# A pre-norm attention and mixture-of-experts kernel on one core: GpSimd's scatters of the last two batches and the last batch's routing in another order, and each tile's two results sent one step sooner

## The chip, the cores and the metric

The kernel runs on one core of a Trainium2 chip. Five engines work side by side and wait for each other by semaphores: TensorE (PE, matmuls), VectorE (DVE), ScalarE (ACT), GpSimd (POOL) and SyncE (SP, which here only issues transfers). The metric is the device time of one execution in microseconds (us), lower is better.

## The reference

The input is four sequences of 1024 tokens of 128 numbers. A layer norm, an attention whose scores are the normalised rows times themselves (scaled by two vectors), and a residual; then a second layer norm and a mixture of 8 experts, of which each token uses two; and a second residual.

```python
x = x + attn(layernorm(x))            # softmax(lhs @ rhs^T) @ x, x: (4, 1024, 128)
xf = layernorm(x).reshape(4096, 128)
probs = softmax(xf @ router_w.T)      # 8 experts
topk_probs, topk_idx = top_k(probs, 2); topk_probs /= sum(topk_probs)
h = gelu(einsum('nc,ech->neh', xf, w_fc) + b_fc)     # hidden 512
out = einsum('neh,ehc->nec', h, w_proj) + b_proj
y = einsum('nec,ne->nc', out, combine)               # combine: the two gates, else 0
x = x + y
```

The kernel computes each token for its two experts alone.

## The kernel before, in words

The tokens are 32 groups of 128 rows, eight to a batch, and a batch (b = 0 to 3) is one sequence. Everything is unrolled code for each engine, with the order of its instructions written out by hand; there is no scheduler. An engine runs its list in order, so an instruction that waits holds back all that stand behind it.

**Attention.** For a batch, TensorE computes 16 blocks of scores (score), VectorE takes their row maxima (row_max), TensorE turns and subtracts them, ScalarE exponentiates (exponent), and TensorE sums the rows in 16 pieces (attend). The last two pieces need shift_again of VectorE and then exponent of ScalarE. While batch b is in work, what is left of batch b - 1 is done beside it: its second layer norm (take_stats2 and take_moments2 on VectorE, scale_ln2 on GpSimd with a power function, make_h2 and high_h2 on ScalarE, split_h2 on VectorE) and its routing.

**Routing.** VectorE finds the two best experts of each row (picks, 11 small steps and a last one that writes "taken"), and the gap of their logits (find_gap, which needs scale_ln2). TensorE counts ranks (rank_round) and VectorE keeps them (keep_ranks). GpSimd raises e to the gap (gate_powers). VectorE's find_slots writes each row's slot and its gates; in the middle it waits for gate_powers (gate_exp). There are five rounds: batch 0, batch 1, the two halves of batch 2 (rounds 2 and 3), batch 3 (round 4, "last"). Then GpSimd sends the rows to their slots in DRAM (dispatch(b, i), i from 0 to 15, an indirect DMA of 128 rows each, a scatter from here on). A dispatch waits for split_h2 of its half (h2lo_made) and find_slots of its round (meta_made). In batch 2 and, before the change, in batch 3, some scatters also wait for a certain maximum or exponent (dispatch_max, dispatch_next, dispatch_own with their PACE numbers), which spreads them.

**Experts.** 39 tiles of 256 slots follow. For tile k, SyncE loads the slots, TensorE turns them (turn_slots), ScalarE copies them (copy_xT), TensorE multiplies by the first weights (up, 12 matmuls), ScalarE does the gelu, TensorE multiplies by the second weights (down, 16 matmuls), VectorE adds the bias and applies the gates (add_bias, gate), and GpSimd sends the 256 results back with two indirect DMAs (give_back). In step k, TensorE does turn_slots(k + 2), up(k), down(k - 2), and VectorE keep_rows(k), add_bias(k - 3), gate(k - 3). up(k) counts the semaphore "stepped"; most engines are paced by it. Tiles 0 to 7 need batches 0 and 1 in their slots, tiles 8 to 15 also batch 2, the rest all. Which slots a tile has is computed by VectorE in three tables (steps(second_table, n) does the next n small steps of the second). In the first steps of this stage the end of the routing still runs: batch 3's round 4, scale_ln2(6) and scale_ln2(7), the scatters of batch 2 and of batch 3 (LAST_SCATTERS says before which step). At the end SyncE waits for all results, loads them, VectorE adds them to x, and SyncE stores.

TensorE goes into the experts after its last attend and a wait for the weights' low parts (low_part on GpSimd, three of them in the last batch).

## Time and profile before

| | us |
|---|---|
| median of 3 runs (lowest, highest) | 371.75 (371.2, 372.22) |
| the profiled execution's own time | 370.49 |
| its span, first to last instruction | 368.7 |
| TensorE busy with matmuls | 293.3 (80%) |
| VectorE, ScalarE, GpSimd busy | 222.1, 194.5, 185.7 |

The span lies 1.8 us below the time of its execution, and that execution 1.3 us below the median. Busy time of TensorE is of pipelined matmuls with modelled ends, so it shows when the engine had work, not that it ran at its best. Attention lasts until 174 us of the span, the experts from there to 347, and the final sum to the end. Times below are from the span's start.

### The profile page before, as it was taken

The numbers are of one execution on the slowest core, as the hardware profiler recorded it, in microseconds if no ns is written. First come the engines' busy times: TensorE is split into PE (matmuls) and PEld (weight loads), VectorE is DVE, ScalarE is ACT, GpSimd is POOL, SyncE is SP. The second block draws the span as 40 slices with busy tenths as digits, with TensorE's granted clock in tenths as the row PEclk, the third lists the DMA queues.
The fourth block names the chain that finished last, engine by engine and source line by source line (L and its number), as shares of the span: only waits on it lengthen the run. The fifth ranks groups of instructions, "written<-read, shape, count | busy, mean of one in ns | idle before, by whom it ended". The sixth has DMA issues, their size and how long they took to land.

```text
span 368.7 us, 7888 instructions
## 1 busy us (share of the span) xinstructions
PE 293.3 (80%) x2206; PEld 256.7 (70%) x2207; DVE 222.1 (60%) x890; ACT 194.5 (53%) x392; POOL 185.7 (50%) x247
## 2 busy tenths in 40 slices
PE   8989988999769994999699272999999999995000
PEld 3669985889558883788588161999999999995000
DVE  3759788888837887778667022665544544453055
ACT  4445557862635614746588022677776777772000
POOL 7011034543865137488786675456555655566300
PEclk9999999999998999999989776799999999999555
DMA  7920000030010001014213321023322222111198
GB/s 218 431 95 1 2 1 0 3 117 16 22 51 29 4 16 45 29 32 118 75 38 90 81 75 59 30 74 110 89 81 75 80 80 72 45 37 50 48 338 325
DMA packets 16948, 29.37 MB, mean 80 GB/s; under 512 B 3760, under 2 KB 12848, under 8 KB 16656
## 3 DMA queue, kind: packets, MB, share of 16 engines
q1 hardware_dynamic: 12080, 18.40, 15.5%
q0 software_dynamic: 4832, 10.53, 8.6%
q8 instruction: 17, 0.28, 0.3%
q14 instruction: 19, 0.16, 0.1%
HBM read 16.30 MB, written 12.62 MB: 78 GB/s over the span
## 4 chain that ended last, share of the span: by engine, by line
PE 60%; DVE 15%; issue 11%; DMA 4%; POOL 4%; ACT 3%; another core or an unknown queue 2%; SPq 1%; POOLq 0%; ACTq 0%; DVEq 0%
PE av_ps L1295 18%; PE av_ps L1094 12%; DVE neg_piece L1402 6%; PE sc_ps L1276 5%; PE sc_ps L1274 5%; PE sc_ps L1275 5%; DMA raw_proj<-results 3%; PE bank L1262 3%; POOL results L867 2%; PE bank L1079 1%; PE sc_ps L1083 1%; PE bank L1083 1%; PE bank L1070 1%; DVE stats L1445 1%
## 5 line engine op out<-in xcount | busy, mean ns | idle before, releaser
L867 POOL DMA_INDIRECT results<-prob,result_row x78 | 75.2, 964 | 57.1 <-PE sc_ps L1276 35.3
L1295 PE MATMUL av_ps<-raw_proj,raw_fc 128*128 x624 | 80.9, 284 | 10.1 <-issue 10.1
L768 POOL DMA_INDIRECT slots<-stage,slot x64 | 63.1, 987 | 45.7 <-DVE stage L1562 21.9
L1295 PEld LDWEIGHTS av_ps<-raw_proj,raw_fc 128*128 128x128 f32 x624 | 76.8, 200 | 10.6 <-issue 9.9
L1011 ACT ACTIVATE raw_fc<-sc_ps,bfc,scale_down 128x256 f32<-128x256 f32 x156 | 75.3, 570 | 2.3 <-PE sc_ps L1276 2.3
L1094 PE MATMUL av_ps<-h_all,prob 128*128 128x137 f32 x512 | 73.2, 287 | 0.0
L1094 PEld LDWEIGHTS av_ps<-h_all,prob 128*128 128x128 f32 x512 | 67.3, 192 | 3.6 <-DVE res L1430 1.1
L1731 DVE TENSOR_TENSOR h_all<-av_ps,bpr 128x256 f32<-128x256 f32 x39 | 16.6, 425 | 75.3 <-PE sc_ps L1276 43.6
L1003 ACT ACTIVATE h_all<-bank 128x512 f16<-128x512 f16 x39 | 23.2, 597 | 60.1 <-PE sc_ps L1276 32.6
L1274 PE MATMUL sc_ps<-h_all,wfc_hi 128*128 128x256 f16 x156 | 43.7, 280 | 2.7 <-issue 1.8
L1275 PE MATMUL sc_ps<-h_all,wfc_hi 128*128 128x256 f16 x156 | 43.7, 280 | 1.1 <-issue 1.1
L1276 PE MATMUL sc_ps<-h_all,wfc_lo 128*128 128x256 f16 x156 | 43.7, 280 | 0.8 <-issue 0.8
L1402 DVE TENSOR_REDUCE neg_piece<-bank 128x1 f32<-128x512 f32 x32 | 21.9, 686 | 16.7 <-remote 6.2
L916 ACT ACTIVATE prob<-sc_ps 128x512 f32<-128x512 f32 x32 | 18.4, 599 | 13.5 <-PE sc_ps L1083 11.3
L906 ACT ACTIVATE again<-bank 128x512 f32<-128x512 f32 x16 | 9.5, 594 | 29.1 <-DVE neg_piece L1402 25.7
L1402 DVE TENSOR_REDUCE neg_piece<-sc_ps 128x1 f32<-128x512 f32 x32 | 21.8, 684 | 0.8 <-issue 0.7
L1738 DVE TENSOR_SCALAR prob<-h_all,row_gate 128x128 f32<-128x128 f32 x78 | 21.5, 385 | 1.4
L1262 PE MATMUL bank<-ident,slots_in 128*128 128x128 f16 x156 | 16.0, 223 | 6.9 <-issue 5.9
L1274 PEld LDWEIGHTS sc_ps<-h_all,wfc_hi 128*128 x156 | 15.6, 100 | 5.2 <-issue 3.1
L1262 PEld LDWEIGHTS bank<-ident,slots_in 128*128 128x128 f16 x156 | 12.0, 99 | 10.1 <-issue 9.6
L1070 PE MATMUL bank<-hT_hi,q_hi 128*128 128x512 f32 x32 | 15.2, 475 | 4.7 <-ACT again L906 4.3
L1276 PEld LDWEIGHTS sc_ps<-h_all,wfc_lo 128*128 x156 | 15.7, 100 | 4.5 <-issue 2.3
(177 smaller groups left out, 516.7 us busy)
## 6 DMA issues: line engine op xcount, KB each, us to landing
slots_in<-slots SPq DMA_DIRECT2D x39, 132.0 KB
raw_fc<-in_w_fc_dram SPq DMA_DIRECT2D x1, 2048.0 KB, 11.2
raw_proj<-in_w_proj_dram SPq DMA_DIRECT2D x1, 2048.0 KB, 15.4
raw_fc<-results SPq DMA_DIRECT2D x2, 1024.0 KB, 7.1
raw_proj<-results SPq DMA_DIRECT2D x2, 1024.0 KB, 11.7
out_dram<-res SPq DMA_DIRECT2D x4, 512.0 KB, 5.0
res<-in_x_dram SPq DMA_DIRECT2D x3, 512.0 KB, 5.6
results<-prob,result_row POOLq DMA_INDIRECT x78
```

Of the source, the lines that this page charges most:

```text
L768: pool.indirect_dma_start(out=slots[:, :], out_offset=bass.IndirectOffsetOnAxis(ap=slot[:, n, k:k + 1], axis=0), in_=stage[:, b % 2, t, :] ...
L867: pool.indirect_dma_start(out=results[:, :], out_offset=bass.IndirectOffsetOnAxis(ap=result_row[a][:, h:h + 1], axis=0), in_=gated[a][h], ...
L1003: act.activation(xT[:, a % NH, :], bank[a % 2][:, :].bitcast(F16)[:, 0:2 * W], ACT.Copy).then_inc(xT_made, 1)
L1011: ins = act.activation(hid[:, a % NH, c, :], up_ps(a, c), ACT.Gelu_apprx_tanh, bias=bfc[:, e, c:c + 1], scale=scale_down[:, 0:1])
L1094: mm = pe.matmul(att[:, t, 0:AUG], probT[:, m % RING, t * P:(t + 1) * P], h_aug[:, b % 2, exp_rows(n), :], start=(n % BT == 0 and t % 2 == ...
L1262: mm = pe.transpose(o[:, part * W + h * P:part * W + (h + 1) * P], x, ident16[:, :])
L1274: pe.matmul(o, wfc_hi[:, e, w], xT[:, a % NH, 0:W], start=True, stop=False, skip_group_check=True)
L1275: pe.matmul(o, wfc_hi[:, e, w], xT[:, a % NH, W:2 * W], start=False, stop=False, skip_group_check=True)
L1276: mm = pe.matmul(o, wfc_lo[:, e, w], xT[:, a % NH, 0:W], start=False, stop=True, skip_group_check=True)
L1295: mm = pe.matmul(o, hid[:, a % NH, c, s], wpr[:, e, c, :], start=(c == 0 and h == 0), stop=(c == HC - 1), skip_group_check=True)
L1402: dve.tensor_reduce(neg_piece[:, r // TU, r % TU, c:c + 1], block_bank(n), AX_X, ALU.max, negate=True).then_inc(max_made, 1)
L1738: ins = dve.tensor_scalar(gated[k % NR][h], biased[:, a % NH, h, :], row_gate[:, a, h:h + 1], None, ALU.mult)
```

## The change

GpSimd's list in the last batch (b = 3): the scatters 5 to 15 of batch 1 no longer wait for maxima or exponents; the first scatters of batch 2 (0 to 7) stand before the weights' low parts instead of behind them; the second power of the gates (round 3) stands behind the low parts instead of ahead of them; scatters 8 to 15 of batch 2 stand in pairs between the remaining small operations. Batch 3's first eight scatters stand before step 4 instead of step 6, the second eight before step 6 instead of step 7. The results of tile k are sent in GpSimd's step k + 3 instead of k + 4. The last batch's routing: VectorE does all steps of picks at once, ahead of its last layer norm statistics and of the tiles; TensorE's rank_round stands behind up(1) instead of behind down(2); keep_ranks stands in step 1 and find_slots in step 2 instead of both in step 5; the second table and split_h2 move with them.

```diff
                 if b == B - 1:
-                    dispatch_max(b - 2)
+                    for i in range(len(PACE_OWN), SCATTERS - 4):
+                        dispatch(b - 2, i)
                     gate_powers(ROUNDS_BY[b - 1] - 2)
-                    dispatch_next(b - 2, 0)
+                    for i in range(SCATTERS - 4, SCATTERS):
+                        dispatch(b - 2, i)
+                    for i in range(2):
+                        dispatch(b - 1, i)
                 if b >= 1:
                     scale_ln2(2 * b - 1)
...
-                if b >= 2:
+                if b == 2:
                     dispatch_next(b - 2, 1)
-                if b >= 1:
-                    gate_powers(ROUNDS_BY[b - 1] - 1)
                 if b == B - 1:
+                    for i in range(2, SCATTERS // 2):
+                        dispatch(b - 1, i)
                     for i in range(EMPTY_PIECES, PIECES):
                         low_part(i)
+                if b >= 1:
+                    gate_powers(ROUNDS_BY[b - 1] - 1)
...
-            for i in range(5):
+            for i in range(8, 10):
                 dispatch(B - 2, i)
             scale_ln2(2 * B - 2)
-            for i in range(5, 11):
+            for i in range(10, 12):
                 dispatch(B - 2, i)
             scale_ln2(2 * B - 1)
-            for i in range(11, 15):
+            for i in range(12, 14):
                 dispatch(B - 2, i)
             gate_powers(len(ROUNDS) - 1)
-            for i in range(15, SCATTERS):
+            for i in range(14, SCATTERS):
                 dispatch(B - 2, i)
...
-            LAST_SCATTERS = {6: range(0, 8), 7: range(8, SCATTERS)}
+            LAST_SCATTERS = {4: range(0, 8), 6: range(8, SCATTERS)}
...
-                if k >= 4:
+                if k >= 3:
                     if tile_there(k):
                         pool.wait_ge(stepped, up_at(k))
-                    give_back(k - 4, (k - 4) % NR)
-            run_each_tile(no_experts, step, 4, lambda group: None)
+                    give_back(k - 3, (k - 3) % NR)
+            run_each_tile(no_experts, step, 3, lambda group: None)
...
             def down(k, a, of, last):
                 e = of
                 pe.wait_ge(gelu_done, k + 1)
-                if isinstance(k, int) and k == 0:
-                    pe.wait_ge(res_made, 2 * B)
-                    pe.wait_ge(lgpart_made, 2 * B)
-                if isinstance(k, int) and k == 3:
+                if isinstance(k, int) and k == 1:
                     pe.wait_ge(ranks_kept, len(ROUNDS))
...
                 if tile_there(k):
                     up(k, a)
+                if isinstance(k, int) and k == 1:
+                    pe.wait_ge(res_made, 2 * B)
+                    pe.wait_ge(lgpart_made, 2 * B)
+                    rank_round(len(ROUNDS) - 1)
                 if later(k, 2):
                     down(k - 2, (a - 2) % NB, expert[a - 2], not tile_there(k + 1))
-                if isinstance(k, int) and k == 4:
-                    pe.wait_ge(biased_made, 2)
-                    rank_round(len(ROUNDS) - 1)
...
             last = len(ROUNDS) - 1
-            choose = picks(last)
+            steps(picks(last), 2 * K * E)
+            take_stats2(2 * B - 1)
+            take_moments2(2 * B - 1)
...
-                if k == 0:
-                    take_stats2(2 * B - 1)
-                    take_moments2(2 * B - 1)
-                if 1 <= k < 4:
-                    steps(choose, (5, 5, 3)[k - 1])
-                if k == 3:
+                if k == 1:
                     find_gap(last)
+                    keep_ranks(last)
+                if k == 2:
+                    find_slots(last)
                     split_h2(2 * B - 2)
                 if k < 5:
-                    steps(second_table, (3, 4, 4, 2, 20)[k])
-                if k == 5:
-                    keep_ranks(last)
-                    find_slots(last)
-                if k == 7:
+                    steps(second_table, (3, 3, 3, 6, 20)[k])
+                if k == 6:
                     split_h2(2 * B - 1)
```

How GpSimd's list reads in the last batch, from the scatters of batch 1 on. L768 is a scatter into slots, L777 the gates' power (gate_powers), L728 to L737 one scale_ln2, L742 the low parts. Before:

```order
L768 DMA slots<-stage,slot 32768x132 x6
L777 TENSOR_TENSOR gate<-euler,gap 128x4
L768 DMA slots<-stage,slot 32768x132 x4
L728 TENSOR_SCALAR neg_mean<-moments 128x4
L734 TENSOR_TENSOR rstd<-var,minus_half 128x4
L737 TENSOR_TENSOR shift<-neg_mean,rstd 128x4
L768 DMA slots<-stage,slot 32768x132 x4
L777 TENSOR_TENSOR gate<-euler,gap 128x4
L742 TENSOR_TENSOR wfc_lo<-raw_fc,wfc_hi 128x512 x3
L768 DMA slots<-stage,slot 32768x132 x5
```

Of the change, the same place:

```order
L768 DMA slots<-stage,slot 32768x132 x10
L777 TENSOR_TENSOR gate<-euler,gap 128x4
L768 DMA slots<-stage,slot 32768x132 x6
L728 TENSOR_SCALAR neg_mean<-moments 128x4
L734 TENSOR_TENSOR rstd<-var,minus_half 128x4
L737 TENSOR_TENSOR shift<-neg_mean,rstd 128x4
L768 DMA slots<-stage,slot 32768x132 x6
L742 TENSOR_TENSOR wfc_lo<-raw_fc,wfc_hi 128x512 x3
L777 TENSOR_TENSOR gate<-euler,gap 128x4
L768 DMA slots<-stage,slot 32768x132 x2
```

Eight more scatters stand ahead of the second of these powers than before (22 instead of 14 from the list's first row on), and the low parts too.

GpSimd's list at batch 3's scatters, behind the last one of batch 2; L867, in the change L874, is a result sent back (give_back). Before:

```order
L768 DMA slots<-stage,slot 32768x132
L867 DMA results<-prob,result_row 20224x128 x4
L768 DMA slots<-stage,slot 32768x132 x8
L867 DMA results<-prob,result_row 20224x128 x2
L768 DMA slots<-stage,slot 32768x132 x8
L867 DMA results<-prob,result_row 20224x128 x72
```

Of the change:

```order
L768 DMA slots<-stage,slot 32768x132 x2
L874 DMA results<-prob,result_row 20224x128 x2
L768 DMA slots<-stage,slot 32768x132 x8
L874 DMA results<-prob,result_row 20224x128 x4
L768 DMA slots<-stage,slot 32768x132 x8
L874 DMA results<-prob,result_row 20224x128 x72
```

One tile's results moved from ahead of batch 3's first eight scatters to behind them. The rows don't show the step each group waits for: the first eight now stand before step 4, the second before step 6.

VectorE's list behind the second tile's keep_rows (its last row is L1724, in the change L1731): in between stands what precedes the third tile's. Before, picks and the second table (L484 to L493):

```order
L1724 TENSOR_TENSOR result_row<-chosen_row,spare_row 128x2
L1511 SCALAR_TENSOR_TENSOR lg<-pick,lg 128x64
L1494 TENSOR_REDUCE best<-lg 128x8
L1497 TENSOR_TENSOR pick<-lg,best 128x64
L1500 SCALAR_TENSOR_TENSOR pick<-pick,expert_id 128x64
L1504 TENSOR_REDUCE first_id<-pick 128x8
L484 TENSOR_REDUCE sums<-chosen 128x16
```

Of the change, find_slots and split_h2 (L1470):

```order
L1731 TENSOR_TENSOR result_row<-chosen_row,spare_row 128x2
L1549 TENSOR_TENSOR pick<-pick,rank 128x64 x2
L1552 TENSOR_REDUCE slot_f<-pick 128x8 x2
L1555 CAST slot<-slot_f 128x16
L1557 TENSOR_SCALAR gate_sum<-gate 128x8
L1561 RECIPROCAL stage<-gate_sum 128x8
L1563 TENSOR_TENSOR stage<-stage,gate 128x8
L1566 TENSOR_SCALAR stage<-first_id 128x8
L1567 COPY stage<-row_id 128x8
L1470 TENSOR_TENSOR stage<-h,stage 128x4x128
```

Before, find_slots stood behind two tiles' add_bias; now it stands ahead of the first tile's. L1557 is the row that waits for the gates' power.

## Rows read from the trace of the kernel before

**Rows 1.** The page: the chain that ended last, by engine.

```profile
PE 60%; DVE 15%; issue 11%; DMA 4%; POOL 4%; ACT 3%; another core or an unknown queue 2%; SPq 1%; POOLq 0%; ACTq 0%; DVEq 0%
```

**Rows 2.** Stretches: busy time and count of each engine, granted clock, DMA share.

```profile
205.00:210.00 5.00, 1.07 (x4) 0.39 (x3) 0.00 (x0) 0.00 (x0) 3.78 (x5) 0.73 0.33 80
...
260.00:300.00 40.00, 39.83 (x384) 37.87 (x383) 18.82 (x95) 28.63 (x60) 22.67 (x24) 1.00 0.29 82
```

**Rows 3.** Timeline of GpSimd (POOL), last batch: start, us, what, idle before.

```profile
138.79 1.07 POOL L768 DMA_INDIRECT slots<-stage,slot  x1 [0.54 <-issue]
...
146.24 1.05 POOL L777 TENSOR_TENSOR gate<-euler,gap 128x4 f32<-128x4 f32 x1
...
156.77 0.19 POOL L728 TENSOR_SCALAR neg_mean<-moments 128x4 f32<-128x4 f32 x1 [1.86 <-DVE moments L1453]
...
158.84 1.07 POOL L768 DMA_INDIRECT slots<-stage,slot  x1 [0.56 <-issue]
...
164.79 3.40 POOL L742 TENSOR_TENSOR wfc_lo<-raw_fc,wfc_hi 128x512 f16<-128x512 f32 x3
```

**Rows 4.** Timelines, last batch: ScalarE's copy of turned maxima; VectorE's find_slots, last shifts.

```profile
146.95 0.60 ACT L902 ACTIVATE neg_rows<-bank 128x512 fp32r<-128x512 f32 x1 [0.86 <-PE bank L1079]
...
154.33 0.68 DVE L1465 TENSOR_TENSOR stage<-h,stage 128x512 f16<-128x512 f32 x1
...
168.77 0.16 DVE L1552 TENSOR_SCALAR gate_sum<-gate 128x4 f32<-128x4 f32 x1
...
169.54 1.28 DVE L1407 TENSOR_TENSOR again<-again,bank 128x512 f32<-128x512 f32 x2
```

**Rows 5.** Timeline of TensorE, the last 64 matmuls of attention.

```profile
166.63 7.76 PE L1094 MATMUL av_ps<-h_all,prob 128*128 128x137 f32 x64
```

**Rows 6.** Timelines in batch 2: GpSimd, TensorE, ScalarE, VectorE.

```profile
96.37 1.08 POOL L768 DMA_INDIRECT slots<-stage,slot  x1 [0.55 <-issue]
...
106.64 0.96 POOL L768 DMA_INDIRECT slots<-stage,slot  x1 [0.30 <-issue]
...
103.15 0.48 PE L1083 MATMUL bank<-neg_rows,ones_r 128*128 128x512 f32 x1
...
107.86 0.60 ACT L916 ACTIVATE prob<-bank 128x512 f32<-128x512 f32 x1 [4.16 <-remote]
...
110.76 0.69 DVE L1402 TENSOR_REDUCE neg_piece<-bank 128x1 f32<-128x512 f32 x1 [6.18 <-remote]
```

**Rows 7.** Timelines of the first tiles: ScalarE, TensorE.

```profile
185.77 0.60 ACT L1003 ACTIVATE h_all<-bank 128x512 f16<-128x512 f16 x1 [3.32 <-PE sc_ps L1276]
...
193.34 1.95 PE L1295 MATMUL av_ps<-raw_proj,raw_fc 128*128 x16
195.81 0.21 PE L1118 MATMUL av_ps<-taken,before 128*128 128x80 f16 x1 [0.52 <-issue]
```

**Rows 8.** Timelines of VectorE and GpSimd, last batch's routing.

```profile
181.51 0.23 DVE L1497 TENSOR_TENSOR pick<-lg,best 128x64 f32<-128x64 f32 x1
...
191.21 1.68 POOL L777 TENSOR_TENSOR gate<-euler,gap 128x8 f32<-128x8 f32 x1
```

**Rows 9.** Timelines of the seventh to tenth tile: TensorE, GpSimd, ScalarE.

```profile
203.91 0.27 PE L1295 MATMUL av_ps<-raw_proj,raw_fc 128*128 x1 [0.66 <-issue]
...
230.16 2.70 PE L1295 MATMUL av_ps<-raw_proj,raw_fc 128*128 x11 [1.03 <-issue]
...
212.88 0.96 POOL L867 DMA_INDIRECT results<-prob,result_row  x1 [2.34 <-remote]
...
227.06 0.96 POOL L867 DMA_INDIRECT results<-prob,result_row  x1 [0.30 <-issue]
```

**Rows 10.** Timelines of the end: GpSimd, VectorE.

```profile
332.31 0.96 POOL L867 DMA_INDIRECT results<-prob,result_row  x1 [1.01 <-PE sc_ps L1276]
...
344.45 0.96 POOL L867 DMA_INDIRECT results<-prob,result_row  x1 [1.44 <-issue]
...
342.75 0.42 DVE L1731 TENSOR_TENSOR h_all<-av_ps,bpr 128x256 f32<-128x256 f32 x1 [2.72 <-remote]
```

More of the change, by code:

```diff
@@ L826, in _ @@
                         store_empty(half)
-                if b >= 2:
+                if b == 2:
                     dispatch_next(b - 2, 1)
+                if b == B - 1:
+                    for i in range(2, SCATTERS // 2):
+                        dispatch(b - 1, i)
+                    for i in range(EMPTY_PIECES, PIECES):
+                        low_part(i)
                 if b >= 1:
                     gate_powers(ROUNDS_BY[b - 1] - 1)
-                if b == B - 1:
-                    for i in range(EMPTY_PIECES, PIECES):
-                        low_part(i)
                 if b >= 1 and b + 1 < B:
```

## The prediction

> **What bounds the kernel now.** I read the chain that ended last first: TensorE has 60% of it [rows 1]. The stretches say where TensorE doesn't work. From 260 to 300 us it is busy 39.83 of 40 us with 384 matmuls [rows 2]; a tile has 32 (4 turns, 12 up, 16 down), so a tile takes 3.33 us and any delay before that stretch is paid in full. From 205 to 210 us, in the seventh tile, it did 4 matmuls and ScalarE and VectorE nothing at all, while GpSimd sent scatters without a break [rows 2]. So the change is decided in three places: the end of attention (until 174 us), the first tiles, and the last results.
>
> The timelines show what a long unbroken run of scatters does. In batch 2 GpSimd sends nine from 96.37 to 107.60 us; TensorE's matmul for an exponent stands at 103.15, yet ScalarE starts that exponent at 107.86, and VectorE waits 6.18 us until 110.76, just after the next scatter [rows 6]. From 203.91 to 212 and again from 219 to 230.16 TensorE advances one matmul at a time, with waits of 0.66, 1.03 and more ahead of single ones that the view calls "issue" [rows 9]. I call this a hold: it begins 5 to 7 us into a run of scatters and ends within about 2 us of its end. Pairs with gaps show none. The Trainium skill says, in "SBUF — State Buffer", section "SBUF: two separate sides", that TensorE and ScalarE have ports of their own and never wait for anyone, and DMA and engines can't slow each other; by that alone there are no holds to move. The trace shows the engines standing beside the scatters, so I keep the hold as an observed pattern, not a port's effect.
>
> **End of attention, +5.6 us.** A scatter in a run takes 0.96 us and a gap of 0.30 [rows 6], with its own start 1.27. The last batch's run starts at 138.79 [rows 3]. Now ten stand in a row: to 151.5. The power (1.05) ends at 152.6, six more scatters (7.6) at 160.2, scale_ln2 takes 2.07 (156.77 to 158.84), six more end at 169.9, the low parts (3.4 to 3.6) at 173.4, and the second power at 174.5 [rows 3]. Before, VectorE used that power at 168.77 [rows 4]. From there it took 2.05 us to the end of the last shift (169.54 + 1.28) [rows 4]; then an exponent (0.60 [rows 6]) and one attend (7.76 / 8 = 0.97 [rows 5]): TensorE ends at 178.1 instead of 174.39 [rows 5], +3.7. This wait alone is certain from the order.
>
> The unbroken ten are like batch 2's nine. A hold from about 145 until 151.5 meets TensorE's turn of the maxima, which came just after 146.2 before (ScalarE used it at 146.95 [rows 4]; I take 151.6), +4.6. Then find_slots' and split_h2's rows for batch 2, ready at 154.93 [rows 4], come at 159.6; the two scatters behind them end at 162.1, scale_ln2 at 164.1, six scatters at 171.7, low parts at 175.3, power at 176.4, and 3.6 later attention ends at 180.0: **+5.6**. Its bounds are +3.7 and, with a second hold in the later six, about +8.
>
> **First tiles, −1.9 us.** Before, six scatters run from 176.82, and ScalarE waits 3.32 us at 185.77 for a signal of a matmul long done [rows 7]. In pairs between other work this goes: −3.3. TensorE's wait of 0.52 for rank_round in step 4 [rows 7] and one of 0.35 behind it go: −0.9; in step 1 "taken" is there in time (attention's end 180.0, its sum and logits 1.7, twelve steps of 0.25: 184.8; TensorE needs it at 185.6). New is a wait of down(2). VectorE: 184.8, statistics 1.5, GpSimd's scale_ln2 2.0, two scatters 2.5, the power 1.7 [rows 8] (192.6), then find_slots' rest 1.1, split_h2 0.7, nine table steps of 0.2, keep_rows twice 1.4, add_bias 0.45: 198.0. TensorE wants it at 193.34 [rows 7] − 174.4 − 3.3 + 180.0 = 195.7: +2.3. Sum −1.9; the seventh tile starts at +3.7. Picks moved ahead cost nothing else: VectorE has idle time there.
>
> **Batch 3's scatters, +2.0 us.** Batch 2's end at 195.2 (194.04 before). The first result goes at 198.6, and 24 scatters of 1.27 follow until 229.1, against 228.02 before [rows 9]. Before, one wait of 2.34 us for "stepped" parted the runs [rows 9], and TensorE did two tiles between the holds. Now the gives behind the first eight are of tiles 1 and 2, which wait for matmuls done before a hold starts (about 204); nothing parts the run. Then TensorE leaves the hold up to two tiles behind, at +1.1: 2 × 3.33 + 1.1 = +7.7 instead of +3.7. A run of 24 is longer than any in the trace, so between +3.7 and +7.7 I take the middle, +5.7 in all.
>
> **Last results, −2.0 us.** In the steady stretch GpSimd now waits for the gates, 1.3 us after "stepped"; two scatters (2.5) of 3.33 us still fit, so nothing is added. At the end GpSimd sends from 332.31 on five tiles' results; VectorE's last bias addition comes at 342.75 after a wait of 2.72, the last two results go from 344.45 on, to 346.67 [rows 10]. With one tile less to send then, the run starts at 333.4 with tile 35, and the last pair ends at 343.5 if no hold meets the last down: −3.2. If the last down is slow for its own reason, the last gate stays at 343.7: 0. I take −2.0, since the run left of the last two tiles is shorter.
>
> **Sum.** 5.6 − 1.9 + 2.0 − 2.0 = +3.7. On the profiled execution's 370.49 that is 374.2; the median lies 1.26 above that execution, so **375.4**.
>
> **Rivals.**
> - *Faster: the holds are parted.* If a gap of some 2 us opens behind batch 3's first eight scatters (a give that must wait for "stepped"), the second hold, 219.3 to 230.16, in which about 8.5 us are lost, goes: 3.7 − 8.5 − 2.0 = −6.8, 365. For it: a gap of 2.34 us was enough before [rows 9]. Against: the gives there are of tiles done. 0.17.
> - *No change: absorbed.* TensorE catches up as the scatters end at +1.1 whatever came before: 1.1 − 2.0 = −0.9, 371. Against: the tiles not done before the run must still be done. 0.12.
> - *Code loading.* The single-matmul stretches are the engine waiting for its instructions, at fixed places of its code; they stay with the tile. Then only the late power counts: +3.7 − 0.9, no wait of down(2), tail 0: +2.8, 374.5. For it: the label "issue". Against: ScalarE's and VectorE's waits in batch 2 for signals of matmuls that the trace has [rows 6]. The Trainium skill, "Runtime: NRT & Kernel Launch", section "Instruction fetch mechanics", says instructions are refilled in blocks by the engine's own DMA queue while it runs; by that rule it is this rival. 0.15.
> - *Holds in full.* The run of 24 costs the two tiles, the six from 164 make another hold (3.3), the last wait gives 1.1 alone: 7.7 + 3.3 − 1.1 = +9.9, 381.5. 0.16.
> - *The forecast,* 0.40, own range 372.5 to 378.5.
>
> **Numbers.** A difference of 0.3% (1.1 us) is what a measurement of this kernel can tell. Faster: 0.17, and 0.04 of the absorbed, 0.02 of the forecast: 0.23. Same: 0.08 of the absorbed and 0.01 of code loading: 0.09. The rest, 0.68, slower. The range leaves out the faster rival and little more: 369.5 to 381.5.
>
> **What the changed kernel's profile would show.** The late power: VectorE's gate_sum row of round 3 behind a wait, at 174 or later, with GpSimd's power just ahead of it. The hold in the last batch: ScalarE's copy of the turned maxima at 151 or later instead of 146.95; if it stands near 147, holds aren't made by long runs. Attention's 64 matmuls end near 180. ScalarE's waits in the first three tiles are under 1 us. The first add_bias is near 198 with TensorE idle ahead of down(2). Batch 3's scatters end near 229, and the number of ups done by then says how much the hold took. The last result ends 2 to 3 us closer to the last up. I am wrong if attention ends on time (the power isn't waited for), or if the stretch from 203 to 230 has one hold less.

## The result, and the profile after

The changed kernel takes **394.75 us** (median of 4 runs, 391.84 to 397.14) where the kernel before took 371.48 beside it (370.97 to 372.22): ratio 1.0621, 95% interval 1.0535 to 1.0708. It is slower, as forecast, but by 23 us and not by 3.7. The profiled execution took 396.4 us, with a span of 394.6. One execution further below, of pool_list_only at 379.97 us, was in a slower state; without it that kernel's median is 376.70 and not 378.02.

The page: first its busy shares, then the chain that ended last, by engine, then the two groups whose idle time is new.

```profile
PE 307.8 (78%) x2206; PEld 263.0 (67%) x2207; DVE 223.9 (57%) x890; ACT 193.0 (49%) x392; POOL 185.3 (47%) x247
...
DVE 31%; PE 23%; another core or an unknown queue 22%; issue 10%; DMA 4%; POOL 4%; ACT 3%; DVEq 1%; SPq 1%; POOLq 0%; ACTq 0%
...
L1738 DVE TENSOR_TENSOR h_all<-av_ps,bpr 128x256 f32<-128x256 f32 x39 | 16.6, 425 | 90.0 <-remote 74.6
L1010 ACT ACTIVATE h_all<-bank 128x512 f16<-128x512 f16 x39 | 23.4, 603 | 74.6 <-remote 63.3
```

TensorE had 60% of the chain [rows 1] and now has 23%; "another core or an unknown queue" rose from 2% to 22%. There is one core. The label, and "remote" in the other rows, stands where the view finds no releaser near the end of a wait, because TensorE had been done for long.

The stretches: the last tiles' part, where TensorE was busy 39.83 of 40 us [rows 2], is no longer full.

```profile
190.00:250.00 60.00, 41.45 (x302) 34.67 (x300) 26.49 (x142) 27.61 (x60) 35.57 (x39) 0.77 0.19 58
250.00:345.00 95.00, 88.67 (x807) 79.55 (x805) 40.79 (x209) 56.94 (x121) 47.76 (x50) 1.00 0.24 69
```

807 matmuls in 95 us are 25.2 tiles of 32, 3.77 us each (3.33 before), at a granted clock of 1.00 as before, so this is no matter of the clock. Timelines of two tiles there: GpSimd, ScalarE, VectorE, TensorE.

```profile
292.54 0.96 POOL L874 DMA_INDIRECT results<-prob,result_row  x1 [3.02 <-DVE result_row L1731]
...
296.34 0.96 POOL L874 DMA_INDIRECT results<-prob,result_row  x1 [0.30 <-issue]
300.29 0.96 POOL L874 DMA_INDIRECT results<-prob,result_row  x1 [2.99 <-DVE result_row L1731]
...
292.84 0.62 ACT L1010 ACTIVATE h_all<-bank 128x512 f16<-128x512 f16 x1
...
298.30 0.60 ACT L1010 ACTIVATE h_all<-bank 128x512 f16<-128x512 f16 x1 [3.02 <-remote]
...
298.57 0.42 DVE L1738 TENSOR_TENSOR h_all<-av_ps,bpr 128x256 f32<-128x256 f32 x1 [4.50 <-remote]
299.03 0.48 DVE L1745 TENSOR_SCALAR prob<-h_all,row_gate 128x128 f32<-128x128 f32 x2
...
294.79 0.27 PE L1283 MATMUL sc_ps<-h_all,wfc_lo 128*128 128x256 f16 x1
294.90 1.95 PE L1298 MATMUL av_ps<-raw_proj,raw_fc 128*128 x16
...
298.20 0.28 PE L1283 MATMUL sc_ps<-h_all,wfc_lo 128*128 128x256 f16 x1 [0.44 <-issue]
```

TensorE's last matmul of an up starts at 294.79, but ScalarE goes on at 298.30, 1.00 us after GpSimd's fourth result in a row (296.34 + 0.96). That is the prediction's hold, now once in every two tiles. The trace's semaphore records say what is held: the update of "stepped" for that up comes at 298.28, while TensorE has gone on with 16 matmuls of a down and more, and ScalarE's own update for its gelu comes at 295.29, in the middle of the run. In this stretch it is TensorE's signal that is held; TensorE itself stops here for 0.44 us alone, in the middle of the next up, where its list has no wait.

The hold feeds itself. The run lasts 4.76 us, and ScalarE and VectorE are released some 1.0 to 1.3 us later. VectorE, with two tiles waiting for it, has the first one's gates applied at 299.51 (299.03 + 0.48), and 0.78 us later, at 300.29, GpSimd starts again. (The view names result_row at the end of that wait. Those row numbers are of a later tile; give_back waits for the gates, by gated_made.) While GpSimd sends that pair, the second tile's results get ready, and four go in a row. One turn of two tiles is 7.75 us, 3.87 a tile. Before, GpSimd waited for TensorE's up and sent two, a pair of 2.2 us in each tile.

Where the 25.9 us of span were added, by ScalarE's copies that open the tiles (the first, the seventh, the twelfth and the last; the before column is absolute, the others are differences from it; each profile is one execution):

```
                     before    after   lag3_only  lag4_rest  pool_list_only  routing_only
first tile           176.02    +12.6     +0.8       +8.0        +6.9           +0.1
seventh tile         194.84    +10.3     +0.2       +5.7        +4.5           +2.7
twelfth tile         235.33    +12.2     +6.1       +3.7        +3.9           +1.0
last tile            325.59    +27.5    +22.6       +3.7        +3.9           +1.0
end of the span      368.70    +25.9    +19.4       +3.5        +3.4           +1.2
```

In this profile half of the delay stands before the first tile, 15.3 us come in the steady stretch, and the tail gives 1.6 back. The first half isn't what the early edits cost in the end: lag4_rest and pool_list_only start their tiles 8.0 and 6.9 us late and end 3.5 and 3.4 late, and lag3_only, nearly on time at the seventh tile, is 6.1 late at the twelfth.

The last batch. Timelines: ScalarE, VectorE, GpSimd and TensorE.

```profile
146.60 0.60 ACT L909 ACTIVATE neg_rows<-bank 128x512 fp32r<-128x512 f32 x1 [0.41 <-issue]
...
155.94 0.60 ACT L923 ACTIVATE prob<-bank 128x512 f32<-128x512 f32 x1 [3.16 <-remote]
...
176.54 0.60 ACT L909 ACTIVATE neg_rows<-bank 128x512 fp32r<-128x512 f32 x1 [5.90 <-PE bank L1086]
...
171.24 4.04 DVE L1423 TENSOR_TENSOR neg_cols<-neg_max,neg_cols 128x4 f32<-128x4 f32 x1
...
181.64 0.16 DVE L1557 TENSOR_SCALAR gate_sum<-gate 128x4 f32<-128x4 f32 x1
...
150.42 0.96 POOL L768 DMA_INDIRECT slots<-stage,slot  x1 [0.30 <-issue]
...
171.87 3.37 POOL L742 TENSOR_TENSOR wfc_lo<-raw_fc,wfc_hi 128x512 f16<-128x512 f32 x3
175.62 1.04 POOL L777 TENSOR_TENSOR gate<-euler,gap 128x4 f32<-128x4 f32 x1 [0.38 <-DVE gap L1531]
...
180.26 7.99 PE L1101 MATMUL av_ps<-h_all,prob 128*128 128x137 f32 x64
```

The copy of the turned maxima is on time (146.95 in [rows 4]). The exponents are late, from the fourth on (155.94 against 153.08 before, after a wait of 3.16 that ends while scatters are still being sent, until 157.48), and the second power is there (175.62 + 1.04) 5 us before VectorE uses it, at 181.64. Attention ends at 188.25, against 174.39 [rows 5].

The first tiles: GpSimd's two runs with batch 3's scatters, and ScalarE behind them.

```profile
206.83 0.96 POOL L874 DMA_INDIRECT results<-prob,result_row  x1 [3.83 <-DVE prob L1745]
...
220.75 0.96 POOL L874 DMA_INDIRECT results<-prob,result_row  x1 [0.30 <-issue]
224.43 0.96 POOL L874 DMA_INDIRECT results<-prob,result_row  x1 [2.73 <-PE sc_ps L1283]
...
238.35 0.96 POOL L874 DMA_INDIRECT results<-prob,result_row  x1 [0.30 <-issue]
...
222.44 0.60 ACT L1010 ACTIVATE h_all<-bank 128x512 f16<-128x512 f16 x1 [14.51 <-remote]
...
240.70 0.60 ACT L1010 ACTIVATE h_all<-bank 128x512 f16<-128x512 f16 x1 [12.48 <-remote]
```

Two runs of twelve, parted by a wait of 2.73, as one of 2.34 parted them before [rows 9]. The run of 24 didn't come about. The long holds also cost TensorE its clock, here as before: the granted clock is 0.69 from 222 to 240 us and 0.58 from 240 to 247 (1.2 GHz, the lower of its two levels, for much of it), and the down at 242.19 takes 3.77 us for 16 matmuls, where the one at 294.90 takes 1.95 at the full 2.4 GHz.

### The profile page after: what moved, and what is told of

Read it like the earlier page. It is cut to its first block, busy times and chain, and to the rows that moved or that the text cites. A ratio compares the mean times of both kernels' runs of the same rounds, so it can differ in the third digit from the quotient of the medians.

```text
span 394.6 us, 7888 instructions
## 1 busy us (share of the span) xinstructions
PE 307.8 (78%) x2206; PEld 263.0 (67%) x2207; DVE 223.9 (57%) x890; ACT 193.0 (49%) x392; POOL 185.3 (47%) x247
## 4 chain that ended last, share of the span: by engine, by line
DVE 31%; PE 23%; another core or an unknown queue 22%; issue 10%; DMA 4%; POOL 4%; ACT 3%; DVEq 1%; SPq 1%; POOLq 0%; ACTq 0%
PE av_ps L1101 8%; DVE neg_piece L1407 6%; DVE h_all L1738 4%; PE av_ps L1298 3%; DVE prob L1745 3%; DMA raw_proj<-results 3%; POOL slots L768 1%; DVE neg_cols L1423 1%; ACT raw_fc L1018 1%; PE bank L1090 1%; PE bank L1086 1%; PE sc_ps L1090 1%; DVE chosen_row L1727 1%; DVE stats L1450 1%
## 5 line engine op out<-in xcount | busy, mean ns | idle before, releaser
L874 POOL DMA_INDIRECT results<-prob,result_row x78 | 75.1, 962 | 74.6 <-DVE result_row L1731 39.7
L1298 PE MATMUL av_ps<-raw_proj,raw_fc 128*128 x624 | 84.2, 291 | 11.3 <-DVE h_all L1738 10.4
L1298 PEld LDWEIGHTS av_ps<-raw_proj,raw_fc 128*128 128x128 f32 x624 | 78.7, 205 | 16.6 <-issue 15.9
L768 POOL DMA_INDIRECT slots<-stage,slot x64 | 62.9, 983 | 54.6 <-DVE stage L1567 21.9
L1101 PE MATMUL av_ps<-h_all,prob 128*128 128x137 f32 x512 | 75.6, 293 | 0.0
L1101 PEld LDWEIGHTS av_ps<-h_all,prob 128*128 128x128 f32 x512 | 70.4, 199 | 3.8 <-DVE res L1435 1.1
L1281 PEld LDWEIGHTS sc_ps<-h_all,wfc_hi 128*128 x156 | 15.5, 100 | 8.8 <-issue 6.6
L1282 PEld LDWEIGHTS sc_ps<-h_all,wfc_hi 128*128 x156 | 15.6, 100 | 6.5 <-issue 5.1
L923 ACT ACTIVATE prob<-bank 128x512 f32<-128x512 f32 x16 | 9.5, 596 | 17.0 <-PE bank L1090 9.1
```

The costliest lines, as they stand in the source:

```text
L768: pool.indirect_dma_start(out=slots[:, :], out_offset=bass.IndirectOffsetOnAxis(ap=slot[:, n, k:k + 1], axis=0), in_=stage[:, b % 2, t, :] ...
L874: pool.indirect_dma_start(out=results[:, :], out_offset=bass.IndirectOffsetOnAxis(ap=result_row[a][:, h:h + 1], axis=0), in_=gated[a][h], ...
L923: act.activation(probT[:, m % RING, :], exp_source(n), ACT.Exp).then_inc(exp_made, 1)
L1101: mm = pe.matmul(att[:, t, 0:AUG], probT[:, m % RING, t * P:(t + 1) * P], h_aug[:, b % 2, exp_rows(n), :], start=(n % BT == 0 and t % 2 == ...
L1281: pe.matmul(o, wfc_hi[:, e, w], xT[:, a % NH, 0:W], start=True, stop=False, skip_group_check=True)
L1282: pe.matmul(o, wfc_hi[:, e, w], xT[:, a % NH, W:2 * W], start=False, stop=False, skip_group_check=True)
```

## The experiments

The kernels of a group ran on one chip, beside the kernel before. Most groups had a chip where that takes 371 us; two had chips where it takes 340, and only the verdicts within a group are compared.

### The change in parts (kernel before here 370.85)

**lag3_only**: the kernel before with the step alone.

```diff
-                if k >= 4:
+                if k >= 3:
...
-                    give_back(k - 4, (k - 4) % NR)
-            run_each_tile(no_experts, step, 4, lambda group: None)
+                    give_back(k - 3, (k - 3) % NR)
+            run_each_tile(no_experts, step, 3, lambda group: None)
```

> The kernel before with one edit: a tile's two results are sent in GpSimd's step k + 3 instead of k + 4. Theory A (the step itself makes a new pattern in the steady stretch: GpSimd starts its two scatters 1.3 us later, they then overlap TensorE's next signal, which is held until they end): tiles take about 3.9 us instead of 3.33 and about 14 us are added, some 385. Theory B (my prediction's term: the step costs nothing in the steady stretch and gives 2 us at the end; the changed kernel's slow tiles come from the late scatters of batch 3): 369.5 to 371.

Measured 388.98 us, ratio 1.0491 (1.0432 to 1.0550). The step alone costs 18.1 us.

**lag4_rest**: the changed kernel with those lines as before.

> The changed kernel with the results sent in step k + 4 again, all else as changed. Theory A: the steady stretch is back at 3.33 us a tile and only the late end of attention stays, about 12 us: 381 to 385. Theory B (the tile pattern comes from the other edits): still above 392.

Measured 375.55, ratio 1.0157 (1.0086 to 1.0228): +4.7. The two together make 22.8 of the whole change's 23.3; they add up. Theory A of the step holds; the 10 to 14 us that it expected here, from the late first tile, did not come.

**pool_list_only**: the kernel before with GpSimd's list of the last batch and the pairs behind it as changed. **routing_only**: the rest, that is the last batch's routing on VectorE and TensorE and batch 3's scatters before steps 4 and 6, with results sent four tiles late as before.

> The kernel before with GpSimd's list alone as changed (last batch and the pairs behind it; batch 3's scatters before steps 6 and 7 as before, routing and results as before). If the late end of attention (12 us) comes from this list: 380 to 385, with the first exponents late from the fourth on and VectorE's small operation beside the low parts at 4 us. If it needs the routing too: under 375.

> The kernel before with the last batch's routing alone as changed on VectorE and TensorE, and batch 3's scatters before steps 4 and 6; GpSimd's list ahead of them and the results as before. Attention ends at 174 us as before. If the routing is harmless: 370 to 373. If its waits (ranks in step 1, the power in step 2) count, as my prediction's 2.3 us for the second weights' wait: 373 to 377.

Measured 378.02, ratio 1.0217 (1.0146 to 1.0288), and 370.34, ratio 0.9991 (0.9953 to 1.0028). The reordered list costs 5.9 to 7.2 us, less than the 9 to 14 expected, and is the whole of the second loss; the routing and the new place of batch 3's scatters cost nothing that the interval (1.7 us less to 1.0 more) would show.

### Why the step costs 18 us

Rival A: the results start so late in a tile that TensorE's signals fall into their run, and are held. Rival B: with a lag of three (a result sent three tiles late instead of four) the waits of GpSimd, VectorE and TensorE close a ring that is too tight, whatever the chip does.

**lag4_timed** sends results four tiles old, and starts them when a lag of three would:

```diff
+                    pool.wait_ge(gated_made, min(k - 2, NTILES))
                     give_back(k - 4, (k - 4) % NR)
```

**lag3_one** and **lag3_memset** have the lag of three, with one result a tile, and with a fill in place of each result. Both leave part of the work out, so their final sum reads rows of the input instead:

```diff
-                for h in range(H):
+                for h in range(1):
                     pool.indirect_dma_start(out=results[:, :],
```

```diff
-                    pool.indirect_dma_start(out=results[:, :],
+                    pool.memset(prob[:, NR * H * D:NR * H * D + 1280], 0.0).then_inc(returned[a], 1)
```

First they ran where the kernel before takes 339.74:

> The kernel before, results of tile k - 4 sent in step k as before, but GpSimd waits in that step until tile k - 3 is gated, as the change makes it. Theory A (what costs is when the two scatters start: 1.3 us after TensorE's signal, they run past its next one 3.33 us later, which reaches the others only when they end): about 3.9 us a tile and 385 to 390, though no result is sent sooner. Theory B (what costs is that results are sent sooner, or one step's data less in between): 3.33 us a tile and 371 to 372.

> The kernel before with step k + 3, and only the first of a tile's two results is sent; at the end the sum reads rows of x in place of the results, in transfers of the same size. Half of the results' scatters are left out. Theory A: one scatter (1 us) from 1.3 us after the signal ends before the next signal, so the steady stretch is at 3.33 us a tile; the span is below 370 also because GpSimd's queue is shorter at the end (some 360 to 366). Theory C (the wait for the gates, not the length of the run, costs): 3.9 us a tile.

> The kernel before with step k + 3, each scatter of a result replaced by GpSimd writing zeros to an unused part of a buffer for about 1.1 us; no result is sent, and the end's sum reads rows of x. If it is the scatters (their descriptors or transfers) that hold TensorE's signals: 3.33 us a tile in the steady stretch. If any work of GpSimd at that time costs: 3.9 us a tile.

Measured 341.79 (ratio 1.0054, 1.0031 to 1.0078), 333.67 (0.9809, 0.9757 to 0.9861) and 340.57 (1.0029, 1.0001 to 1.0057). On that chip none of them costs 18 us; the bare step wasn't run there. The expectations, made for a kernel of 371, missed. The traces show why: from the tenth tile on lag4_timed makes one in 3.32 us (once 4.12), and the first tiles wait in one place only. The holds are nearly absent there.

The same three and the bare step, where the kernel before takes 371.56:

> Before with the results' lag of three tiles alone, again, now beside the others of this call. Theory H (TensorE's signals to other engines wait for the end of a run of GpSimd's scatters, and the pair of results then falls where the signals are due): where the kernel before takes about 371 us, 389 again; on a chip where it takes about 340, as in the last call, and where its tiles pass without holds, within 1 us of the kernel before. Theory W (GpSimd with a lag of three closes a cycle of waits with VectorE and TensorE whatever the chip): 15 to 20 us over before on either chip.

> Before with results of tile k-4 that also wait until tile k-3 is gated, so that they start when those of a lag of three would. Theory H: where before takes about 371, 385 to 390; where before takes about 340, within 2 us of it. Theory W: within 1 us of before on either chip, since what VectorE waits for of GpSimd is a tile older.

> A lag of three with one of each tile's two results sent; the final sum reads rows of the input instead, so half of the results is left out. Theory H: the runs are half as long, so where before takes about 371 the excess over it is at most a third of lag three's 18 us (under 377, and well under if a scatter's share of the hold is what counts); where before takes about 340, some 6 us below it as before. Theory W: 12 us or more over before.

> A lag of three in which each result's scatter is a fill of 1.1 us on GpSimd instead, and the final sum reads rows of the input; none of the results is sent. Theory H: no scatter, no hold in the steady stretch, so no more than 2 us over before where that takes about 371, likely some us below it. Theory W: GpSimd is as long busy and as late, 12 us or more over before.

| kernel | us | ratio to before | twelfth to last tile, us |
|---|---|---|---|
| before | 371.56 | | 90.26 (its profile above) |
| b_lag3_only | 391.07 | 1.0517 (1.0477 to 1.0556) | 106.93 |
| b_lag4_timed | 387.71 | 1.0446 (1.0412 to 1.0480) | 105.99 |
| b_lag3_one | 360.24 | 0.9707 (0.9673 to 0.9742) | 90.26 |
| b_lag3_memset | 354.10 | 0.9518 (0.9480 to 0.9557) | 93.62 |

Timeline of b_lag4_timed in the steady stretch: GpSimd, then ScalarE.

```profile
274.71 0.96 POOL L867 DMA_INDIRECT results<-prob,result_row  x1 [3.08 <-PE sc_ps L1277]
...
278.49 0.96 POOL L867 DMA_INDIRECT results<-prob,result_row  x1 [0.30 <-issue]
282.54 0.96 POOL L867 DMA_INDIRECT results<-prob,result_row  x1 [3.09 <-PE sc_ps L1277]
...
275.05 0.62 ACT L1004 ACTIVATE h_all<-bank 128x512 f16<-128x512 f16 x1
...
280.58 0.60 ACT L1004 ACTIVATE h_all<-bank 128x512 f16<-128x512 f16 x1 [3.09 <-remote]
```

Four results in a row, then ScalarE 1.13 us behind the last (278.49 + 0.96): the pattern of the changed kernel, with results of four tiles' distance. So it is the start that costs, not the distance: B expected this kernel within 1 us of the one before. The same late start costs 2.1 us on the other chip. With one result a tile the stretch takes what it took before; with fills, which keep GpSimd as busy (2.39 us for two), it takes 93.6 us, of which 3.4 are in its first two tiles (4.66 and 5.35), and 3.34 a tile behind them. With the fills B falls a second time: the waits are those of a lag of three, and neither chip shows the 12 us that it expected. The slow stretch needs scatters, and at least two a tile. Whether issuing them or their transfers hold the signals stays open, since a fill leaves out both. The last row says more: without any results scattered, and so with part of the work left out, the kernel is 17.5 us under the one before.

### Why the list costs 5 to 7 us (kernel before here 371.20)

**c_list_paced** paces batch 1's scatters by maxima and exponents again and leaves the low parts and the second power late; **c_powers_first** leaves the run and puts the second power ahead of the low parts. The first had run as list_paced where the kernel before takes 339.74.

> The kernel with GpSimd's list alone as changed, but the scatters 5 to 15 of batch 1 wait for maxima and exponents again, as before the change. If the unbroken ten hold TensorE's signals, the exponents of the last batch are back near their old times (the fourth at 153 instead of 154, the fifth at 155 instead of 160), and what stays is the power behind the low parts: attention ends 3 to 4 us late instead of 7, total 373 to 376. If the run is not the cause: as the list alone, 378.

> Before with the changed order of GpSimd's list in the last batch and of the slots' scatters behind it, again, beside the two that undo a piece of it. Where before takes about 371: 376 to 379, as before.

> The same with batch 1's scatters paced by VectorE's maxima and ScalarE's exponents again, the low parts and the second power as changed. If the unbroken run of batch 1's scatters costs the 7 us (TensorE's scores are seen late by ScalarE), it is within 2 us of the kernel before where that takes about 371. If the late low parts and power cost them, it stays 5 to 8 us over.

> The changed list with the second power ahead of the three low parts. If the late power is what is waited for, 3 to 7 us under the changed list alone; if the unbroken run of batch 1's scatters or the low parts beside VectorE are, within 1 us of it.

Measured: list_paced 347.24 (1.0211, 1.0157 to 1.0264), which is 7.5 us more even where the holds hardly show, with a wait of 6.06 us ahead of ScalarE's last two exponents; on the third chip c_pool_list 377.64 (1.0156, 1.0113 to 1.0199), c_list_paced 376.83 (1.0145, 1.0118 to 1.0172), c_powers_first 375.30 (1.0121, 1.0076 to 1.0165). Undoing either piece gives back 0.8 and 2.3 us of the 6.4: each that is left costs most of what both do. In c_list_paced, timelines of ScalarE and VectorE:

```profile
158.50 0.60 ACT L924 ACTIVATE prob<-sc_ps 128x512 f32<-128x512 f32 x1 [1.27 <-PE sc_ps L1091]
...
178.92 1.23 ACT L924 ACTIVATE prob<-again 128x512 f32<-128x512 f32 x2 [6.16 <-DVE again L1415]
...
177.44 0.17 DVE L1560 TENSOR_SCALAR gate_sum<-gate 128x4 f32<-128x4 f32 x1 [0.99 <-POOL gate L777]
```

Seven of the eight exponents are on time (the eighth is at 165.85, 160.71 before, behind the scatters that end the paced run), and now the power is waited for: its gate_sum comes at 177.44 (168.77 in [rows 4]), and ScalarE has the last two exponents after a wait of 6.16 us. In c_powers_first it is the other way round: gate_sum, at 176.55, waits for nothing, and the fourth exponent and the second copy of turned maxima are late (155.68 and 172.85; 153.08 and 164.71 before). Timeline of ScalarE:

```profile
155.68 0.60 ACT L924 ACTIVATE prob<-bank 128x512 f32<-128x512 f32 x1 [3.29 <-remote]
...
172.85 0.60 ACT L910 ACTIVATE neg_rows<-bank 128x512 fp32r<-128x512 f32 x1 [3.19 <-PE bank L1087]
```

With both, the held exponents push VectorE behind the power. Two delays stand side by side, and the longer counts.

### Other versions

**c_spread2**: the kernel before with its last 16 scatters in pairs.

```diff
-            LAST_SCATTERS = {6: range(0, 8), 7: range(8, SCATTERS)}
+            LAST_SCATTERS = {6 + i: range(2 * i, 2 * i + 2) for i in range(8)}
```

> Before with the last batch's 16 scatters sent two a tile with tiles 6 to 13 in place of eight with tile 6 and eight with tile 7. If a hold costs its run's length once and signals pass between runs, a tile takes about 5.1 us (four scatters of 1.27) for eight tiles where the two long runs took 14.7 and 9 us, and the kernel is 3 to 8 us under before where that takes about 371. If GpSimd's total is what counts, the same as before within 2 us.

Measured 374.13, ratio 1.0084 (1.0053 to 1.0114): slower, where a gain was expected. ScalarE's copies stand 6.0 us apart for eight tiles (203.38, 209.48, 215.49, and so on to 245.41): four scatters in a row (5.06 with the gap ahead of each) and about 1 us to the release. So the 5.1 us a tile that was expected lacked the release: shorter runs end more often, and each end costs it again.

**d_lag5** has a lag of five. **d_tail3** has four, and three for the last two tiles and behind them. Both ran where the kernel before takes 339.65, so neither says what it would do beside the long holds.

> Before with the results' lag of five tiles in place of four. The results still start at the end of each tile's up, so theory H expects the steady stretch unchanged at 3.32 a tile and only the tail longer, by one pair of results, 2.5 us: 2 to 3 us over before. If distance alone decides (three is short, so five is safer and faster), it is faster than before.

> Before with a lag of four until the last two tiles and of three from there: the gain that a step sooner was taken to give at the end, without the steady stretch. The prediction's own term for the last results says 2 us under before. If the extra pair holds the last two tiles' signals as in the steady stretch of lag three, 0 to 2 us over instead.

Measured 341.59, ratio 1.0053 (1.0036 to 1.0070), and 339.01, ratio 0.9987 (0.9973 to 1.0002). A step later costs 1.9 us; a step sooner at the end alone is worth 0.6, not told from nothing, where 2 were expected. None of the versions that compute everything beat the kernel before.

## Why the prediction was right in sign and wrong in size

**Last results, −2.0 us: the step that failed.** "Two scatters (2.5) of 3.33 us still fit, so nothing is added" was a term put at nothing that cost 18.1 us alone (lag3_only). It looked at GpSimd's time and not at what a scatter does to the engines' signals. The term at the end was about right: from the last tile's copy to the end of the span it took 43.1 us before, 41.5 after, 39.9 in lag3_only. The steady stretch, put at nothing, costs 15.3 us after, 16.5 in lag3_only. The prediction had the mechanism, the hold, and fenced it in too closely: it "begins 5 to 7 us into a run". In the rows above, TensorE's matmul stands at 294.79, 2.25 us into a run, and its signal is held until the run is over. The sign is right by the smaller part of the loss: the term that made most of it was forecast as a gain. What the pairs of before escaped by was their start at the up's end, and not their length alone: b_lag4_timed moves only that.

**End of attention, +5.6 us.** Attention ends at 188.25 and not at 180.0. The delay at the first tile was +8.0 in lag4_rest, +9.4 in c_pool_list and +12.6 after, with the same order of GpSimd's list up to there. GpSimd's own times came out as worked out, its second power at 176.66 for 176.4. The hold is there, but not where it was put: not on the turned maxima (146.60, not 151.6), but on the fourth exponent (155.94), 2.9 us late, and further on. The prediction's sign, "if it stands near 147, holds aren't made by long runs", was one that the rows of the same run contradict: it looked at a single signal. "This wait alone is certain from the order" is wrong as a sum: in the changed kernel the second power isn't waited for, since VectorE is later than it; c_list_paced shows that it would be. VectorE's neg_cols took 4.04 us beside GpSimd's low parts in that execution and 0.22 in lag4_rest, which can be some of the difference of the two. The Trainium skill ("SBUF — State Buffer", "Who interferes with whom") says that a VectorE instruction with two inputs in SBUF contends with a GpSimd instruction that reads SBUF, by an exclusive lock that goes to whichever starts first. The row agrees that the two contend, as it ends at 175.28 with the third low part (175.24), but not on the order: VectorE's row starts ahead of the first low part (171.24, 171.87) and still lasts through all three. By the same page of the Trainium skill the ports of TensorE and ScalarE are shared with nobody, and DMA shares none with engines; that rule doesn't account for the holds, in which engines wait for signals.

**First tiles, −1.9 us.** From the first tile to the seventh the delay shrinks by 2.3 us, both after and in lag4_rest: about right, and the two main terms are in the trace. The wait of 3.32 at the fourth copy is gone (194.41 has none), and the new wait of down(2), put at +2.3, is there, 2.93 ahead of 205.76. But the terms don't add up over the kernels: routing_only alone loses 2.6 in these tiles, and pool_list_only alone gains the same 2.3.

**Batch 3's scatters, +2.0 us.** From the seventh tile to the twelfth it grows by 1.9 us after, and shrinks by 2.0 in lag4_rest. The run of 24 doesn't exist: a wait of 2.73 for TensorE parts it. So the reason was wrong, and that the size fits the one kernel is luck; routing_only with these scatters moved is at 0.9991.

**The rivals.** Without the step, lag4_rest is +3.7 from the twelfth tile on, inside the forecast's own range. That is partly luck: the first tile was 2.4 us later than forecast, and the stretch behind the seventh gave 2.0 instead of taking 2.0. *Faster* had its gap, 2.73 us, and no gain: ScalarE's wait at the second run is 12.48 us all the same. *Absorbed* falls for the changed kernel, which is as late at the twelfth tile (12.2) as at the first (12.6); lag4_rest absorbs half, 8.0 to 3.7. "Holds in full", +9.9, put more into the same places, and none into the steady stretch. *Code loading* falls: b_lag4_timed differs from b_lag3_only and from the kernel before on GpSimd alone, and b_lag3_one and b_lag3_memset have TensorE's code unchanged; its stalls move by 16 us with GpSimd's scatters. Nor is it loading slowed by the scatters' traffic, at least in the steady stretch: in the changed kernel's trace no packet of the two instruction queues starts between 318.87 and 341.21 us, and there too ScalarE waits 3.02 us until 329.52 and 3.05 until 337.31. What stays open is what in the chip holds TensorE's signals.

## What to carry to other kernels

Before moving transfers that GpSimd issues, look at when in the cycle they start and which engine's signals fall into their run: a pair with 0.3 us between its scatters was harmless at one place of a 3.33 us tile and, on the chips where the kernel takes 371 us, made it 3.87 at another. A start that is tied to the engine whose signals matter (here the up's last matmul) keeps the cycle in step; one tied to what that engine's signals release can lock into a slower one. And if two waits end near one another, undo both before pricing either.

## What the chips showed that was not expected

The same kernel takes 371 us on some chips and 340 on others: 370.85, 371.56 and 371.20 on three, 339.74 and 339.65 on two more, each from repeated runs. The difference stands where the long runs of scatters are. d_lag5, on a chip of 340, has its first tile at 168.20, its twelfth at 207.03 and its last at 297.44: against the kernel before on a chip of 371 that is 7.8 us less up to the first tile, 20.5 less from there to the twelfth, and the same (90.41 and 90.26) in the steady stretch. Why the holds are there on one chip and hardly on another stays open. The late start (lag4_timed) costs 16.2 us on a chip of the first kind and 2.1 on the other. A verdict on an edit that moves GpSimd's scatters holds for the kind of chip that it was measured on. A scatter itself costs the same on both: 0.96 us, and 0.30 to the next.
